# Two attention blocks on one core: VectorE takes over the second normalisation's centring and the sums of squares from ScalarE

## What is computed

```python
h = jnp.maximum(_layernorm(x), 0.0)
x = x + masked_attention(h, adj, W_qkv, b_qkv, W_out, b_out)   # 8 heads of 16
h = jnp.maximum(_layernorm(x), 0.0)                            # the second normalisation
z_l, z_g, v = h @ Wl, h @ Wg, h @ Wv
A_l = relu(cosine similarity of the rows of z_l), no diagonal, lower triangle, rows scaled to sum 1
A_g = exp(-|z_g[n] - z_g[m]|^2 / 2),              no diagonal, lower triangle, rows scaled to sum 1
x = x + (0.9 * A_l + 0.1 * A_g) @ v @ Wo
```

## Time and profile before

| | |
|---|---|
| device time, median of 3 runs (lowest to highest) | 844.66 us (844.1 to 846.99) |
| the profiled execution: its device time / its span | 843.65 us / 841.8 us |
| busy: PE, DVE, ACT, POOL | 89%, 80%, 70%, 74% of the span |
| SBUF mask multiplies of GpSimd (L587) | 488.4 us in 384 operations |

### The profile page before, as it was taken

One profiled execution on the slowest core, in us unless ns is written; L12 is line 12 of the kernel. 1 busy time (PEld: TensorE's weight loads), 2 busy tenths in 40 slices (PEclk: granted clock), 3 DMA queues, 4 the chain that ended last, 5 costly groups with the idle time before them and its releaser, 6 DMA issues.

```text
span 841.8 us, 15492 instructions
## 1 busy us (share of the span) xinstructions
PE 750.9 (89%) x4648; PEld 408.8 (49%) x4724; DVE 671.6 (80%) x1957; ACT 588.8 (70%) x1230; POOL 624.2 (74%) x707
## 2 busy tenths in 40 slices
PE   4777789899998989989898989989898999989886
PEld 3212245546464545546464544645455464636366
DVE  6777769797887979788797979788796978877266
ACT  4456786867768686876768686776868677685832
POOL 3269885978879697887869688886969688696911
PEclk9969899999999999999999999999999999999999
DMA  2312111210201121120202111020112102000000
GB/s 81 100 34 67 42 38 33 70 33 29 74 20 52 33 70 33 38 64 20 72 17 65 32 45 58 21 83 20 51 32 70 33 27 64 21 14 2 13 1 26
DMA packets 43059, 35.76 MB, mean 42 GB/s; under 512 B 6625, under 2 KB 36834, under 8 KB 42978
## 3 DMA queue, kind: packets, MB, share of 16 engines
q1 hardware_dynamic: 42978, 34.76, 13.5%
HBM read 17.70 MB, written 16.78 MB: 41 GB/s over the span
## 4 chain that ended last, share of the span: by engine, by line
PE 55%; DVE 20%; ACT 12%; issue 9%; POOL 1%; SPq 0%; DMA 0%; DVEq 0%; POOLq 0%; ACTq 0%
PE adj L761 14%; PE score L725 10%; PE pv L747 10%; DVE scrap L1021 8%; PE adj L756 7%; PE work L779 6%; ACT probs_t L1186 4%; DVE adj_cos L1039 3%; DVE rbf_arg L1048 3%; DVE adj_rbf L1053 2%; PE work L756 2%; ACT zl_square L1264 2%; PE work L895 2%; ACT z L1257 2%; ACT adj_sb L1264 1%
## 5 line engine op out<-in xcount | busy, mean ns | idle before, releaser
L587 POOL TENSOR_TENSOR probs_t<-probs_t,keep_t 128x512 int32<-128x512 int32 x384 | 488.4, 1298 | 68.6 <-ACT probs_t L1186 68.4
L1186 ACT ACTIVATE probs_t<-turned,exp_scale 128x512 f32<-128x512 f32 x512 | 344.4, 693 | 91.1 <-PE turned L733 88.1
L1021 DVE CUSTOM_DVE_ANT_0 scrap<-score,mask_add 128x512 f32<-128x512 f32 x512 | 340.0, 681 | 49.9 <-PE score L725 49.7
L725 PE MATMUL score<-qk_rows 48*128 48x512 f16 x512 | 192.2, 392 | 43.2 <-ACT probs_t L1186 23.0
L733 PE MATMUL turned<-qk_rows 50*128 50x512 f16 x512 | 191.6, 394 | 1.7 <-ACT probs_t L1186 1.1
L747 PE MATMUL pv<-probs_t,v_cols 128*32 128x512 f32 x1024 | 139.8, 619 | 1.3 <-POOL probs_t L587 1.3
L725 PEld LDWEIGHTS score<-qk_rows 48*128 48x128 f16 x512 | 44.2, 93 | 182.8 <-issue 113.2
L761 PE MATMUL adj<-v_cos,adj_cos 128*128 128x129 f32 x480 | 69.3, 286 | 0.4 <-DVE out_sb L1076 0.4
L761 PEld LDWEIGHTS adj<-v_cos,adj_cos 128*128 128x128 f32 x480 | 58.1, 190 | 21.9 <-issue 21.2
L761 PE MATMUL adj<-z,adj_rbf 128*128 128x129 f32 x480 | 64.6, 278 | 0.0
L1053 DVE SCALAR_TENSOR_TENSOR adj_rbf<-rbf_exp,mask_t 128x512 f32<-128x512 f32 x64 | 61.7, 967 | 1.0 <-ACT rbf_exp L1220 1.0
(11 more groups left out here) (170 smaller groups left out, 1094.7 us busy)
## 6 DMA issues: line engine op xcount, KB each, us to landing
q_dram<-split SPq DMA_DIRECT2D x48, 128.0 KB, 2.1
k_dram<-split SPq DMA_DIRECT2D x48, 128.0 KB, 2.1
qk_rows<-q_dram SPq DMA_DIRECT2D x64, 96.0 KB, 2.6
qk_rows<-k_dram SPq DMA_DIRECT2D x64, 96.0 KB, 2.7
x_sb<-in_x_dram SPq DMA_DIRECT2D x16, 256.0 KB, 3.2
out_dram<-out_sb SPq DMA_DIRECT2D x15, 256.0 KB, 2.5
qk_rows<-max_rows SPq DMA_DIRECT2D x128, 2.0 KB
adj_sb<-in_adj_dram SPq DMA_DIRECT2D x1, 256.0 KB, 3.1
```

Source lines behind the costliest of these rows:

```text
L587: pool.tensor_tensor(tile, tile, keep_t[:, w // HG % T, :], ALU.mult).then_inc(probs_masked.sem, 1)
L725: pe.matmul(score_bank[u % 2][:, :], qk_rows[row:row + ROWS, b % 2, 0, h // 2, t * P:(t + 1) * P], qk_rows[row:row + ROWS, b % 2, 1, h // ...
L1021: dve.tensor_tensor_reduce(scrap[:, u % 2, :], score_bank[u % 2][:, :], mask_add[:, t, :], -1.0 / MAX_UNIT, 3.0e38, ALU.add, ALU.min, neg_ ...
L1186: act.activation(probs_t[:, kept(b, k), w % HG, :], turned_bank[w % 2][:, :], ACT.Exp, scale=exp_scale[:, 0:1]).then_inc(probs_ready.sem, 1)
```

## The change

The second normalisation is taken apart: VectorE makes relu(x1 - mean) (`ln2_centre`), the product z is taken of that, and the row's factor, which is positive and so may pass through relu and the product, is multiplied in when ScalarE copies z. GpSimd's shift (two small operations) and ScalarE's `ln2_scale` go. `z_sums` is on VectorE in all batches. The table AT has new slots; the two tables of the last batches are unchanged.

```diff
 
 AT = {
 
-    "hT": (-26,), "q": (-24,), "k": (-22,), "v": (-13,), "max_turn": (17, 32),
-    "pv": (28, 32, 36, 40, 44, 48, 52, 56), "y": (54, 59), "yT": (60,), "attn": (62,), "h2T": (66,),
-    "z": (69, 70, 72, 74), "zgT": (76,), "col": (78,), "zlT": (79,), "rbf": (79, 83, 85, 87),
-    "cos": (81, 83, 86, 90), "mix_cos": (92, 95, 97, 98), "mix_rbf": (94, 95, 97, 98),
-
-    "ln_scale": (-34,), "hT_copy": (-26,), "q_hi": (-24,), "k_hi": (-22,), "max_copy": (17, 32),
-    "pv_copy": (42, 56), "yT_copy": (60,), "ln2_scale": (65,), "h2T_hi": (66,), "z_copy": (69, 71, 73, 74),
-    "z_sums": (71, 72, 74, 75), "zgT_hi": (75,), "col_copy": (77,), "zlT_hi": (79,), "rbf_exp": (82, 83, 87, 89),
-
-    "ln_moments": (-36,), "hT_split": (-26,), "q_rest": (-24,), "k_rest": (-21,), "v_add": (-12,),
-    "max_split": (14, 28), "y_scale": (57, 59), "x1": (62,), "ln2_moments": (63,), "h2T_lo": (67,),
-    "zgT_lo": (76,), "zlT_lo": (79,), "rbf_read": (78, 83, 85, 87), "cos_read": (81, 83, 87, 90),
-    "rbf_mask": (83, 84, 88, 92), "out": (93, 96, 97, 100),
-
-    "ln_rstd": (-37,), "x_biased": (-28,), "ln2_rstd": (61,), "z_norms": (77,),
-
-    "qk_store": (-37,), "rows": (-9, -6), "x_next": (-18,), "max_load": (8, 24), "store": (92,),
+    "hT": (-29,), "q": (-25,), "k": (-22,), "v": (-13,), "max_turn": (17, 32),
+    "pv": (28, 32, 36, 40, 44, 48, 52, 56), "y": (54, 59), "yT": (60,), "attn": (62,), "h2T": (65,),
+    "z": (67, 68, 69, 71), "zgT": (76,), "col": (78,), "zlT": (79,), "rbf": (79, 83, 85, 87),
+    "cos": (81, 83, 86, 89), "mix_cos": (92, 95, 97, 99), "mix_rbf": (93, 95, 97, 99),
+
+    "ln_scale": (-32,), "hT_copy": (-30,), "q_hi": (-25,), "k_hi": (-22,), "max_copy": (17, 32),
+    "pv_copy": (41, 56), "yT_copy": (60,), "h2T_hi": (65,), "z_copy": (67, 69, 70, 71), "zgT_hi": (76,),
+    "col_copy": (78,), "zlT_hi": (78,), "rbf_exp": (80, 83, 86, 90),
+
+    "ln_moments": (-36,), "hT_split": (-28,), "q_rest": (-24,), "k_rest": (-21,), "v_add": (-12,),
+    "max_split": (14, 29), "y_scale": (57, 59), "x1": (62,), "ln2_moments": (62,), "ln2_centre": (63,),
+    "h2T_lo": (65,), "zgT_lo": (76,), "zlT_lo": (79,), "rbf_read": (78, 83, 85, 87), "cos_read": (81, 82, 86, 91),
+    "rbf_mask": (83, 84, 88, 92), "z_sums": (68, 70, 75, 76), "out": (93, 96, 97, 99),
+
+    "ln_rstd": (-37,), "x_biased": (-12,), "ln2_rstd": (61,), "z_norms": (77,),
+
+    "qk_store": (-26,), "rows": (-21, -7), "x_next": (-22,), "max_load": (-6, 22), "store": (110,),
 }
...
         moments2 = sb("moments2", [P, T, 2])
         var_eps2 = sb("var_eps2", [P, T])
         rstd2 = sb("rstd2", [P, T])
-        neg_mean2 = sb("neg_mean2", [P, T])
-        ln2_shift = sb("ln2_shift", [P, T])
-        x1_norm = sb("x1_norm", [P, T, D])
+        x1_centred = sb("x1_centred", [P, T, D])
         h2T_parts = sb("h2T_parts", [P, 2, N], F32R)
         z = sb("z", [P, T, ZC])
         square_sum = sb("square_sum", [P, T, 2])
...
         ln2_moments = signal("ln2_moments")
         ln2_var = signal("ln2_var")
         ln2_rstd = signal("ln2_rstd")
-        ln2_neg = signal("ln2_neg")
-        ln2_shifted = signal("ln2_shifted")
         ln2_done = signal("ln2_done")
         h2T_filled = signal("h2T_filled")
         h2T_hi = signal("h2T_hi")
...
                 if hit := due(s, "ln2_rstd"):
                     b, _ = hit
                     reached(pool, ln2_moments, b)
-                    reached(pool, ln2_done, b - 1)
+                    reached(pool, z_ready, b - 1)
                     pool.tensor_scalar(var_eps2[:, :], moments2[:, :, 1], LN_EPS, None,
                                        ALU.add).then_inc(ln2_var.sem, 1)
-                    pool.tensor_scalar(neg_mean2[:, :], moments2[:, :, 0], -1.0, None,
-                                       ALU.mult).then_inc(ln2_neg.sem, 1)
                     reached(pool, ln2_var, b)
                     pool.tensor_tensor(rstd2[:, :], var_eps2[:, :], minus_half[:, :],
                                        ALU.pow).then_inc(ln2_rstd.sem, 1)
-                    reached(pool, ln2_neg, b)
-                    reached(pool, ln2_rstd, b)
-                    pool.tensor_tensor(ln2_shift[:, :], neg_mean2[:, :], rstd2[:, :],
-                                       ALU.mult).then_inc(ln2_shifted.sem, 1)
                 if hit := due(s, "x_biased"):
                     b, _ = hit
                     if b == 0:
...
                     b, _ = hit
                     reached(pe, ln2_done, b)
                     bank_free(pe, work_turns, b, "h2T")
-                    turn_tiles(lambda t: x1_norm[:, t, :], h2T_filled)
+                    turn_tiles(lambda t: x1_centred[:, t, :], h2T_filled)
                 if hit := due(s, "z"):
                     b, t = hit
                     reached(pe, h2T_hi, b)
...
                     dve.tensor_tensor_reduce(scrap[:, u % 2, :], score_bank[u % 2][:, :], mask_add[:, t, :],
                                              -1.0 / MAX_UNIT, 3.0e38, ALU.add, ALU.min,
                                              neg_max[:, u // HALF, lane, place:place + 1]).then_inc(max_ready.sem, 1)
-                if (hit := due(s, "z_sums")) and hit[0] == B - 1:
+                if hit := due(s, "z_sums"):
                     b, t = hit
                     reached(dve, z_ready, b, t + 1)
                     if t == 0:
...
                 if hit := due(s, "ln2_moments"):
                     b, _ = hit
                     reached(dve, x1_ready, b)
+                    reached(dve, ln2_var, b - 1)
                     layer_norm_moments(b, lambda t: x1[:, b % 2, t, :], bn2_sb, moments2, ln2_bn, ln2_moments)
+                if hit := due(s, "ln2_centre"):
+                    b, _ = hit
+                    reached(dve, ln2_moments, b)
+                    reached(dve, h2T_filled, b - 1)
+                    for t in range(T):
+                        last = dve.tensor_scalar(x1_centred[:, t, :], x1[:, b % 2, t, :], moments2[:, t, 0:1], 0.0,
+                                                 ALU.subtract, ALU.max)
+                    last.then_inc(ln2_done.sem, 1)
                 if hit := due(s, "h2T_lo"):
                     b, _ = hit
                     reached(dve, h2T_hi, b)
...
                         last = act.activation(x_norm[:, t, :], x_sb[:, t, :], ACT.Relu,
                                               bias=ln_shift[:, t:t + 1], scale=rstd[:, t:t + 1])
                     last.then_inc(ln_done.sem, 1)
-                if hit := due(s, "ln2_scale"):
-                    b, _ = hit
-                    reached(act, x1_ready, b)
-                    reached(act, ln2_shifted, b)
-                    reached(act, h2T_filled, b - 1)
-                    for t in range(T):
-                        last = act.activation(x1_norm[:, t, :], x1[:, b % 2, t, :], ACT.Relu,
-                                              bias=ln2_shift[:, t:t + 1], scale=rstd2[:, t:t + 1])
-                    last.then_inc(ln2_done.sem, 1)
                 if hit := due(s, "max_copy"):
                     b, g = hit
                     reached(act, max_turned, b, g + 1)
...
                 if hit := due(s, "z_copy"):
                     b, t = hit
                     reached(act, z_filled, b, t + 1)
-                    act.copy(z[:, t, 0:3 * D], z_bank(b, t)[:, 0:3 * D]).then_inc(z_ready.sem, 1)
-                if (hit := due(s, "z_sums")) and hit[0] < B - 1:
-                    b, t = hit
-                    reached(act, z_ready, b, t + 1)
                     if t == 0:
-                        reached(act, floor_ready, b - 1)
-                    for a in range(2):
-                        last = act.activation((zl_square, zg_square)[a][:, t, :], z[:, t, a * D:(a + 1) * D],
-                                              ACT.Square, accum_out=square_sum[:, t, a:a + 1])
-                    last.then_inc(sums_ready.sem, 1)
+                        reached(act, ln2_rstd, b)
+                    act.activation(z[:, t, 0:3 * D], z_bank(b, t)[:, 0:3 * D], ACT.Identity,
+                                   scale=rstd2[:, t:t + 1]).then_inc(z_ready.sem, 1)
                 if hit := due(s, "zgT_hi"):
                     b, _ = hit
                     reached(act, zgT_filled, b)
```

## The result

The changed kernel takes **908.21 us** (median of 4 runs, 901.06 to 913.5) against 845.47 for the kernel before, measured beside it: a ratio of 1.0736 (95% interval 1.0659 to 1.0814). The prediction said 871 us with 828 to 883 as its range: the direction was right, the size was not. The profiled execution took 913.5 us, with a span of 911.8 against 841.8.

A forecast was written before the change was run, and what follows sets the result against it. No engine was full; TensorE, ScalarE and VectorE each limited one stretch of the 48.23 us batch. Profiled 843.65 us plus 13.5 batches at +2.1 (28.4), minus 2.1 at the start, gave 869.9, so 871 us; range 828 to 883.

The forecast's parts named there:

- Tile 2's (slot 11) now stand ahead of `k_rest`, on which zgT waits, and behind zgT come col and rbf, one after another: Tile 2's sums on VectorE before the rest of k: nothing hides them, +1.9 us a batch.
- the sum of 2.1 us a batch: Net per batch: -1.1 ScalarE, +0.8 tile 1's sums, +1.9 tile 2's sums, +0.5 second cosine read.
- The price of the sums: VectorE's two sums per tile wait for GpSimd's multiplies: 1.9 us a tile, between 0.43 and 2.29.
- the centrings: Four 128x128 VectorE operations, 1 to 2 us, covered by VectorE's idle time and TensorE's mix products: nothing.
- Tile 1's +0.8: Tile 1's sums in slot 6, ahead of q's rest: 1.9 less 1.04 us of VectorE idle time, +0.8 us.
- The sum's upper end: Sums at 2.29 us a tile in both places: 2.9 us more a batch, 883 us in all.
- z's last product no longer fills the time between k and zgT: That product moved to slot 7, so nothing hides tile 2's sums before zgT; part of the +1.9 us.
- ScalarE's relief, -1.1 us: Sums leaving ScalarE give TensorE back 0.56 us before k and 0.5 us of its 1.2 us wait for exponentials.
- The second cosine read, +0.5 us: Read moved from slot 19 to 18: VectorE idles 0.5 us for the second product in the stretch it sets.
- The start, -2.1 us: First batch: the centring removes TensorE's 2.12 us wait for the scaled rows, once.
- the faster one: Rival: sums do not share GpSimd's path, 0.43 us a tile; 828 to 840 us, taken as 834; chance 0.27.

The follow-up runs named there:

- run 5: Changed kernel, VectorE's sums of squares reading z from PSUM times the row's factor as first input, only the second from SBUF: 843.79 us, ratio 0.9993.
- run 10: run 5 with the second read of the cosine bank moved back from slot 82 to 83: 841.58 us, ratio 0.995.
- run 3: Changed kernel with unread bf16 products on TensorE where it idles, seven before zgT and three before col, batches 1 to 13: 871.00 us, ratio 1.0313.
- run 13: run 5 with VectorE held up on purpose in slot 75 by three further maxima over the score bank, batches 1 to 13: 886.63 us, ratio 1.0496.
- run 4: Changed kernel, same VectorE sum operations and slots, but first input from the score bank in PSUM (results not the reference's), batches 0 to 13: 841.22 us, ratio 0.9973.
- run 8: Changed kernel with z's last product and its copy back in slot 74 instead of 71, sums still on two SBUF inputs: 851.27 us, ratio 1.0093.
- run 2: Kernel before, with only the sums of squares moved to VectorE in all batches, slots 70, 72, 75 and 76: 854.75 us, ratio 1.0116.
- run 7: Changed kernel with the sums back on ScalarE, spread over slots 71, 72, 74 and 75 as in the kernel before: 852.70 us, ratio 1.01.
- run 9: run 5 with z's last product and its copy back in slot 74: 834.88 us, ratio 0.9878.
- run 1: Changed kernel with the sums back on ScalarE in neighbouring slots 69 to 72, all batches but the last: 893.59 us, ratio 1.06.

## Why the prediction was right in direction and wrong in size

Of the 70.0 us by which the span grew, 9.4 lie ahead of the first batch's z_norms (116.81 to 126.24). TensorE's mean clock up to there is 0.80, against 0.90 before. Runs 5 and 10 differ only in a cosine read behind that point, and yet z_norms begins after 115.1 us in the one and after 120.3 in the other. So some 5 us differ from one execution to the next, and how much of the 9.4 the change adds is open. The other 60.6 us lie behind it: from 126.24 to 761.74 twelve batches take 52.96 us each, against 48.48 in the mean of the same twelve before, and 48.23 for an undisturbed one.

- **The step that failed: "Tile 2's (slot 11) now stand ahead of `k_rest`, on which zgT waits, and behind zgT come col and rbf, one after another"**, priced at +1.9 us, and with it the sum of 2.1 us a batch. It counts TensorE's wait and takes what follows at the durations of before. One term was put at nothing without a reason: the fall of the clock behind the wait, which is 2.8 to 2.9 us a batch (runs 3 and 13). The rows for it were there: of the full batches of the kernel before, two take 49.2 instead of 48.2 us at a mean clock of 0.97, and I read the period of an undisturbed one. One of the two:

```profile
384.61:433.80 49.19, 45.99 (x288) 25.43 (x293) 40.59 (x121) 36.28 (x77) 38.22 (x44) 0.97 0.15 44
```

- **The price of the sums: right for tile 2.** I took 1.9 us a tile with 2.29 as the upper end; tile 2 measures 2.43 (439.89 to 442.32), a little over it, and tile 3, where GpSimd had nothing left to multiply, takes 0.28 for each sum. Run 4 shows the reason: the second SBUF input. The Trainium skill (VectorE: DVE Perf Modes, section "Two Vector instructions with no wait between them") names the shared interface; sums and masks agree with it. For the centrings, which I had left contending by that page, no row here decides: they take 0.28 us each, but stand beside small operations of GpSimd on 128x4 and 128x16. They cost nothing, as forecast.
- **What it does to the path: right for tile 2, luck in the sum.** TensorE waits 1.92 us before zgT for the rest of k, in 13 batches; forecast was 1.9. Without the fall of the clock the sum comes out well too, 50.3 us a batch forecast and 50.1 in run 3, but its other three terms (-1.1, +0.8 and +0.5) nearly cancel, and none of them came as priced. Tile 1's +0.8 is not seen: TensorE waits for the rest of q before k only once (0.3 us; before, 8.8 us in 15 times), and run 3's batch is 2.1 us longer than run 5's with the sums nearly free, of which tile 2's wait is 1.9. (The sum's upper end adds up to 882 and not 883.)
- **"z's last product no longer fills the time between k and zgT"**: the move decides between 48.6 and 53 us (run 8), but hardly by the way that I gave. It sets when VectorE's sums meet GpSimd. That it takes work out of TensorE's gap is not shown to cost anything (runs 5 and 9). In the old order the same sums cost 0.7 us a batch (run 2). I priced the sums by GpSimd's mean share of busy time, 0.77; what counts is whether it is busy at that moment.
- **ScalarE's relief, -1.1 us: too much.** With the sums nearly free (runs 4 and 5) the batch takes 48.2 and 48.0 us, where before it took 48.2. Part of the relief is there: with everything else of the change in and the sums on ScalarE (run 7) it takes 48.7, so the sums' leaving is worth 0.5 to 0.7 us. The other parts of the change cost about as much. TensorE's waits for exponentials shrank, and waits of col (0.95 us) came. A gain of half a microsecond over the kernel before appears only with z's last product back in its slot (run 9).
- **The second cosine read, +0.5 us: wrong.** The wait was there (0.45 us), but it was not on the path (run 10).
- **The start, -2.1 us.** TensorE's wait of 2.12 us for the scaled rows is gone, as forecast. In the time it cannot be seen beside the 9.4 us above.
- **The rivals.** The sums do share the path, so the faster one fell. Its time, 834 us, is not what its condition gives: with the sums off the path and nothing else moved, run 5 takes 843.8. Run 9 reaches 834.9 with a move that the change doesn't have.

Open: why the clock falls in one batch and not in the next with the same waits (runs 1 and 13), and how much of the 9.4 us at the start the change adds. Neither was tried further.

## What to carry to other kernels

A wait of TensorE can have two prices: its own length, and the work behind it at half the clock; look at the granted clock of the stretch behind every wait that a change adds or lengthens, and read the slow batches of the kernel before, not only the typical one. On VectorE, an operation on two SBUF inputs beside a busy GpSimd cost here up to a whole operation of GpSimd each, though it was small (1.37 us instead of 0.28); with one input still in PSUM, it cost nothing extra. And a small move in a slot table can decide whether two such operations meet at all.

## What the runs showed of the hardware

- A 128x128 operation of VectorE with two SBUF inputs takes 0.28 us alone and up to 1.37 us beside GpSimd's multiplies of 1.24 us; two in a row pay twice (1.23 and 1.34). GpSimd hardly pays: three multiplies take 3.78 us with two sums between them (1.26 each), while the 128x512 mask cost it 0.5 us.
- With one input in PSUM the same operation takes 0.28 to 0.30 us beside the same multiplies (run 4); with a column as scale, 0.35 (run 5).
- Added work made the kernel faster: ten products a batch that nobody reads, put into TensorE's waits, brought 37 us (run 3).
- A fall of the granted clock to about half, after 1.65 and 0.95 us of idle time in short succession, costs 2.8 us here, and does not come each time (run 13).
